# A graph attention layer's gather-and-sum: edge groups of 512 with 512-column products into separate sums, and softmax denominators by scans

## The chip, the cores and the metric

The kernel runs on one core of a Trainium2 chip. The metric is the device time of one execution in microseconds (us).

## The reference

Nodes have 1024 features in 4 heads of 256. 50,000 edges, sorted by their target node `dst`, run between N = 3125 nodes. The graph layer projects the normalised nodes (`xp`), gives each edge and head a softmax weight, and sums the weighted rows of the sources into their targets. A quantised linear layer follows.

```python
xp = (layernorm(x) @ W).reshape(N, H, C)                 # N=3125, H=4, C=256
e = leaky_relu(a_src[src] + a_dst[dst], 0.2)             # with self loops
m = segment_max(e, dst); ee = exp(e - m[dst])
z = segment_sum(ee, dst)                                 # the denominators
out = segment_sum(xp[src] * (ee / z[dst])[:, :, None], dst) + bias
x = x + relu(out)
x = x + (quantised layernorm(x)) @ (quantised weight).T + bias
```

## The kernel before

There are four stages, each a function with its own program for each engine. `normalise` and `project` make the tables; `aggregate` is the gather-and-sum; `finish` divides by the denominators and runs the linear layer. PE multiplies, DVE and ACT are the vector and scalar engines, POOL issues the gathers, SP issues plain transfers.

`project` writes `d_xp`, one row of 4 KB for each node: 1024 values in float16, and their rest in float16 (the high and the low part). It also makes the edges' weights in a layout with 128 edges on the partitions. Along the edges, it finds each node's largest logit with scans (line 1195 and 1201), writes them to `d_segmax`, and gathers them by node into `nmax` (`gather`, line 1022).

`aggregate` works on chunks of 128 edges. A step is 2 chunks, 256 edges in sorted order; there are 196 of them. Nodes come in 25 tiles of 128. A step whose edges cross from one tile to the next handles those of one tile only, and 24 border steps of one chunk each take the edges left over. So there are 220 steps and 416 chunks, in the order of `PLAN`: 6 border steps first, then a border step after every 10 others. For each chunk:

- POOL gathers 128 rows of `d_xp` into one of 12 buffers `xg` (line 1682). It waits until PE is done with that buffer (semaphore `mm_done`).
- DVE makes a one-hot matrix `hot` of the edges' targets (line 1701) and the low parts of the weights, `wgt` (line 1712); ACT makes the high parts (line 1757), 4 instructions a chunk.
- PE multiplies for each of 4 heads three pairs of parts, 256 columns each, all into the same sums `sum_ps` (line 1783): 12 products a chunk. At the end of a step it multiplies `hot` with the weights themselves, 8 columns, into `z_ps` (line 1793).

After each step DVE adds `z_ps` to the denominators `zsum` (line 1740) and `sum_ps` to the tile's rows in `acc` (line 1741). The queues of each engine are fixed by the order in the code; semaphores tie them together. `sum_ps` has 3 buffers, `z_ps` 2, `wgt` 3.

## Time and profile before

| what | value |
|---|---|
| median of 3 runs | 1515.13 us (1513.52 to 1517.62) |
| the profiled execution's own time | 1526.42 us |
| its span | 1524.7 us |
| main loop of `aggregate`: first product to last sum | 524.2 to 1211.9 us |
| first gather to the start of the last | 519.4 to 1197.6 us |
| granted TensorE clock, mean of the span | 0.96 |

A profile lists when each instruction started and how long it took, and what ended the wait before it. Busy shares of the engines over the whole span are PE 87%, DVE 71%, ACT 66%, POOL 44%. Instructions that issue a gather count as POOL's work. "issue" as the releaser means that the profile shows nothing that the engine waited for.

### The profile page before, as it was taken

The page shows a single profiled execution, that of the slowest core. Times are in us where ns is not written, and L with a number is a line of the kernel's source. Part 1 is how long each engine was busy: PE and PEld are TensorE (multiplying, and loading weights), DVE is VectorE, ACT ScalarE, POOL GpSimd, SP SyncE. Part 2 cuts the span into 40 slices and gives each one's busy share as a digit, 9 for nine tenths or more (in the row PEclk, how much of TensorE's full clock was granted, in tenths as well). Part 3 has the DMA queues.
Part 4 walks back from the last instruction along what each step waited for, and adds up shares of the span by engine and source line. Part 5 has one row for each costly group of instructions (what it writes and reads, how often), then busy time and mean ns, then how long its engine had stood idle before and what let it go on. Part 6 is the DMA issues. An engine that isn't in the chain of part 4 may idle for free. (4 is left out here: it accounts for less than half of the span.)

```text
span 1524.7 us, 29568 instructions
## 1 busy us (share of the span) xinstructions
PE 1327.2 (87%) x10150; PEld 902.0 (59%) x10150; DVE 1081.6 (71%) x2255; ACT 1006.7 (66%) x2253; POOL 672.7 (44%) x610
## 2 busy tenths in 40 slices
PE   7998577899997678889899988888998769999997
PEld 5775244554443367777677777776777634544543
DVE  7997489889833567666676666676676787777771
ACT  3667478885445467777777777776777665666652
POOL 1003411111255466666666566665666244443441
PEclk9999799999998899999999999999999979999999
DMA  6784475543463698988898998988888857767752
GB/s 233 275 297 134 138 251 184 181 157 119 152 215 111 235 317 313 317 310 299 305 309 307 309 349 303 316 301 292 306 309 300 306 162 189 195 173 195 188 141 48
DMA packets 110549, 363.62 MB, mean 238 GB/s; under 512 B 20204, under 2 KB 20988, under 8 KB 110148
## 3 DMA queue, kind: packets, MB, share of 16 engines
q0 software_dynamic: 66048, 225.15, 45.7%
q1 hardware_dynamic: 40996, 135.71, 26.0%
q8 instruction: 82, 1.34, 0.3%
q10 hardware_dynamic: 3360, 0.91, 0.2%
q14 instruction: 63, 0.52, 0.1%
HBM read 299.78 MB, written 72.85 MB: 244 GB/s over the span
## 5 line engine op out<-in xcount | busy, mean ns | idle before, releaser
L1783 PE MATMUL sum_ps<-xg,wgt 128*128 128x256 f16 x4992 | 602.5, 277 | 91.5 <-issue 66.8
L1757 ACT ACTIVATE wgt<-hot,tables 128x128 f16<-128x128 f16 x1664 | 503.0, 388 | 187.8 <-PE sum_ps L1783 61.5
L1783 PEld LDWEIGHTS sum_ps<-xg,wgt 128*128 128x128 f16 x4992 | 475.5, 99 | 185.3 <-issue 112.8
L1682 POOL DMA_INDIRECT xg<-d_xp,tables x404 | 414.1, 1025 | 243.9 <-issue 98.3
L1555 PE MATMUL xp_ps<-acc 128*128 128x512 f16 x1152 | 274.3, 387 | 21.7 <-issue 11.9
L1741 DVE TENSOR_TENSOR acc<-sum_ps,acc 128x1024 f32 x220 | 268.1, 1219 | 1.4 <-issue 1.3
L2180 PE MATMUL fmm_ps<-xg,tables 128*128 128x512 f16 x1200 | 265.0, 381 | 4.0 <-DVE tables L2009 4.0
L2180 PEld LDWEIGHTS fmm_ps<-xg,tables 128*128 128x128 f16 x1200 | 117.8, 98 | 141.8 <-issue 7.1
L1555 PEld LDWEIGHTS xp_ps<-acc 128*128 128x128 f16 x1152 | 108.9, 99 | 146.6 <-issue 28.5
L1740 DVE TENSOR_TENSOR zsum<-z_ps,zsum 128x8 f32 x220 | 35.5, 162 | 217.1 <-PE z_ps L1793 75.4
L1712 DVE TENSOR_TENSOR wgt<-hot,tables 128x512 f16<-128x512 f16 x416 | 157.8, 418 | 0.0
L1911 POOL TENSOR_TENSOR tables<-tables,finv 128x1024 f32<-128x1024 f32 x24 | 45.9, 1912 | 131.8 <-DVE finv L1997 131.8
L1059 POOL TENSOR_TENSOR acc<-acc,q_inv 128x1024 f32<-128x1024 f32 x8 | 17.3, 2157 | 176.1 <-DVE q_inv L1184 176.1
L1532 PEld LDWEIGHTS gat_ps<-table,oh 128*128 128x128 f16 x790 | 41.9, 99 | 60.4 <-issue 25.3
L1532 PE MATMUL gat_ps<-table,oh 128*128 128x100 f16 x790 | 48.8, 210 | 32.5 <-DVEq L1139 19.9
L1131 DVE TENSOR_TENSOR prod<-gat_ps,mask 128x500 f32<-128x500 f32 x79 | 53.2, 674 | 32.3 <-remote 19.4
L1424 ACT ACTIVATE acc<-xp_ps,half_scale 128x1024 f16<-128x1024 f32 x24 | 26.7, 1112 | 70.4 <-PE xp_ps L1555 61.3
L2021 DVE SCALAR_TENSOR_TENSOR tables<-ftr_ps,tables 128x1024 f16<-128x1024 f32 x24 | 29.4, 1225 | 53.1 <-ACT tables L2123 53.1
L1456 ACT ACTIVATE oh<-tables,back_lane 128x1280 f16<-128x1280 bf16 x40 | 54.0, 1351 | 16.0 <-remote 15.6
L1701 DVE TENSOR_TENSOR hot<-iota,tables 128x256 f16<-128x256 f16 (+1 forms) x220 | 59.8, 273 | 3.8 <-PEq L1767 3.7
L1917 POOL TENSOR_TENSOR tables<-fq,fscale 128x1024 f32<-128x1024 fp8e4 x24 | 53.9, 2244 | 14.9 <-ACT fq L2114 14.9
L1153 DVE SCALAR_TENSOR_TENSOR acc<-xp_ps,half_scale,acc 128x1024 f16<-128x1024 f32 x24 | 30.7, 1281 | 41.7 <-ACT acc L1425 24.7
(320 smaller groups left out, 1526.4 us busy)
## 6 DMA issues: line engine op xcount, KB each, us to landing
d_xnT<-acc SPq DMA_DIRECT2D x25, 512.0 KB, 3.6
tables<-d_lo SPq DMA_DIRECT2D x40, 320.0 KB
own_row<-d_own SPq DMA_DIRECT2D x25, 512.0 KB
wdT<-in_x_dram SPq DMA_DIRECT2D x24, 512.0 KB, 5.1
acc<-d_xnT SPq DMA_DIRECT2D x24, 512.0 KB
d_xp<-acc SPq DMA_DIRECT2D x24, 512.0 KB
d_own<-acc SPq DMA_DIRECT2D x24, 512.0 KB
xr<-in_x_dram SPq DMA_DIRECT2D x24, 512.0 KB
```

What stands on the lines that cost most here:

```text
L1131: return own.mark(nc.vector.tensor_tensor(out=prod[:, :, :, :], in0=gat_ps[u % 2][:, 0:UCOLS * V].rearrange("p (c h t) -> p c h t", c=UCOL ...
L1456: nc.scalar.activation(oh[at][:, :], digits[at], ACT.Abs, bias=back_lane[:, :]).then_inc(oh_ready, 1)
L1532: last = nc.tensor.matmul(gat_ps[u % 2][:, c * V:(c + 1) * V], oh[b % LB][:, col], table[a][:, :], start=(c == 0 and a == 0), stop=(c == U ...
L1555: done = nc.tensor.matmul(xp_ps[j][:, cols], xh[j][:, a, c, :], w16[:, c, b, cols], start=False, stop=(c == KC - 1 and a == 1), skip_group ...
L1682: nc.gpsimd.indirect_dma_start(out=xg[s][u][:, :, :].rearrange("p a n -> p (a n)"), out_offset=None, in_=d_xp, in_offset=bass.IndirectOffs ...
L1701: nc.vector.tensor_tensor(out=hot[k % TURN][:, 0:n, :].rearrange("p u (n b) -> p u n b", b=2), in0=iota16[:, :].rearrange("p (n b) -> p n ...
L1712: last = nc.vector.tensor_tensor(out=wgt[k % WB][:, u, HEADS:V, :].rearrange("p v (n b) -> p v n b", b=2), in0=hot[k % TURN][:, u, :].rear ...
L1741: nc.vector.tensor_tensor(out=s_acc, in0=sum_ps[k % SB][:, :], in1=s_acc, op=ALU.add).then_inc(added, 1)
L1757: last = nc.scalar.activation(wgt[k % WB][:, u, h, :], hot[k % TURN][:, u, :], ACT.Copy, scale=col(numT[:, h, :], u, q))
L1783: last = nc.tensor.matmul(sum_ps[s][:, h * C:(h + 1) * C], w[:, u, a * HEADS + h, :], x[u][:, b, h * C:(h + 1) * C], start=(u == 0 and h % ...
L1917: nc.gpsimd.tensor_tensor(out=blocks(xn[t % XN]), in0=blocks(q8[t % 2][:, :]), in1=spread(scale[t % XN][:, :]), op=ALU.mult).then_inc(xq_r ...
L2180: return nc.tensor.matmul(mm_ps[t % 2][:, cols], xqT[t % 2][:, a, c, :], wd[c][:, b, cols], start=False, stop=last, skip_group_check=True)
```

## The change

A step becomes a group of 4 chunks, 512 edges, worked in two parts of 2 chunks (`PARTS`). There are 98 groups. The 24 border pieces become one part each, so 2 chunks where it was 1. In all there are 220 parts and 440 chunks. For each head and chunk, one product of 512 columns takes the weights' high part with both parts of the row, into two separate sums; a second one of 256 columns takes the low part of the weights with the high part of the row. `sum_ps` is now 2048 columns with 2 buffers, and DVE adds both halves into `acc` once per group or border piece.

The products for the denominators and their adds are gone. Instead DVE runs sums along the edges in `project` (`line_sums`, `sum_carries`, `segment_sums`), SP writes them to `d_segsum`, and POOL gathers them by node in `aggregate`, 25 gathers of 16 bytes a row, one behind each of the parts 12 to 36.

```diff
@@ -32,7 +32,8 @@
 LAST_EVEN = LAST_ROWS // 16 * 16
-SUB = 2
+SUB = 4
+PAIR = 2
 ET = -(-E // (SUB * P))
 EC = ET * SUB
 EP = EC * P
@@ -40,14 +41,14 @@
 CROSSES = TILES - 1
 STEPS = ET + CROSSES
 LEAD = 6
-EVERY = 10
+EVERY = 5
 def sequence():
     plan, crosses = [(ET + j, 1) for j in range(LEAD)], LEAD
     for i in range(ET):
-        plan.append((i, SUB))
+        plan.append((i, SUB // PAIR))
         if i % EVERY == EVERY - 1 and crosses < CROSSES:
             plan.append((ET + crosses, 1))
             crosses += 1
@@ -55,8 +56,9 @@
 PLAN = sequence()
-assert len(PLAN) == STEPS and all(n == SUB for _, n in PLAN[-8:])
-KCOLS = 2 * P
+PARTS = [(step, q, w, n) for step, (q, n) in enumerate(PLAN) for w in range(n)]
+assert len(PLAN) == STEPS and all(n == SUB // PAIR for _, n in PLAN[-4:])
+KCOLS = P
 KT = STEPS
 HCOLS = 17
 HBATCH = 24
...
+    d_segsum = nc.dram_tensor("d_segsum", (EP, HEADS), F32, kind="Internal").ap()
...
+                if t == BUSY + 13:
+                    sp.wait_ge(sums_ready, 1)
+                    sp.dma_start(g["d_segsum"].rearrange("(p c) h -> p (c h)", c=EC),
+                                 segmax[:, :, :].rearrange("p c h -> p (c h)")).then_inc(segmax_out, 16)
...
+            sp.wait_ge(segmax_out, 32)
...
-            for c in range(CH):
-                for u in range(SUB):
-                    part = slice(u * P, (u + 1) * P)
-                    gather(srow[:, c, part], halves(d_src), step_i[:, c, u:u + 1], ends_in)
-                    gather(drow[:, c, part], halves(d_dst), step_i[:, c, u:u + 1], ends_in)
+            for part_no in range(SUB // PAIR):
+                part = slice(part_no * PAIR * P, (part_no + 1) * PAIR * P)
+                gather(srow[:, part], pairs(d_src), step_i[:, part_no:part_no + 1], ends_in)
+                gather(drow[:, part], pairs(d_dst), step_i[:, part_no:part_no + 1], ends_in)
             pool.wait_ge(tile_out, 16)
...
-            for c in range(CH):
-                for u in range(SUB):
-                    part = slice(u * P * HEADS, (u + 1) * P * HEADS)
-                    gather(nrow[c][:, part], halves(d_num), step_i[:, c, u:u + 1], rows_in)
+            for part_no in range(SUB // PAIR):
+                gather(w[:, part_no, :], pairs(d_num), step_i[:, part_no:part_no + 1], rows_in)
             highest(range(5, TILES))
...
+            def running_sums(start):
+                for h in range(HEADS):
+                    last = nc.vector.tensor_tensor_scan(segmax[:, :, h], same[:, :], edge[:, :, h], start(h), ALU.mult, ALU.add)
+                return last
+            def line_sums():
+                dve.wait_ge(num_ready, 1)
+                dve.wait_ge(steps_read, 1)
+                running_sums(lambda h: 0.0).then_inc(ends_ready, 1)
+            def sum_carries():
+                dve.wait_ge(sums_turned, 1)
+                own.link(nc.vector.tensor_copy(line_sum[:, 0, :], gat_ps[1][0:HEADS, 0:P]))
+                own.link(nc.vector.tensor_tensor_scan(line_sum[:, 1, :], joined[:, 1, :], line_sum[:, 0, :], 0.0, ALU.mult, ALU.add))
+                nc.vector.memset(line_sum[:, 0, 0:1], 0.0)
+                nc.vector.tensor_tensor(out=line_sum[:, 0, 1:P], in0=line_sum[:, 1, 0:P - 1], in1=joined[:, 0, 1:P],
+                                        op=ALU.mult).then_inc(cin_ready, 1)
+            def segment_sums():
+                dve.wait_ge(cinT_done, 2)
+                dve.wait_ge(sums_turned, 1)
+                own.link(nc.vector.tensor_copy(zcinT[:, :], g_ps[:, 0:HEADS]))
+                running_sums(lambda h: zcinT[:, h:h + 1]).then_inc(sums_ready, 1)
...
+                if t == BUSY + 8:
+                    line_sums()
+                if t == BUSY + 9:
+                    sum_carries()
...
                 if t == BUSY + 12:
                     num_pairs()
                     own_logits()
+                    segment_sums()
...
-    SB = 3
-    ROUND = 12
+    SB = 2
+    COUNT = len(PARTS)
...
-        sum_ps = [ps(f"sum_ps{j}", [P, D]) for j in range(SB)]
-        z_ps = [ps(f"z_ps{j}", [P, 512]) for j in range(2)]
+        hot = [sb(f"hot{j}", [P, PAIR, P], F16) for j in range(TURN)]
+        wgt = [sb(f"wgt{j}", [P, PAIR, V, P], F16) for j in range(WB)]
+        sum_ps = [ps(f"sum_ps{j}", [P, HEADS, 2, C]) for j in range(SB)]
...
+            for p in range(XB, COUNT):
+                gather(p)
+                if ZFROM <= p < ZFROM + TILES:
+                    t = p - ZFROM
+                    nc.gpsimd.indirect_dma_start(
+                        out=zsum[:, t, :], out_offset=None, in_=g["d_segsum"],
+                        in_offset=bass.IndirectOffsetOnAxis(ap=g["last_i"][:, t:t + 1], axis=0)).then_inc(g["z_in"], 16)
...
+            def add(p):
+                step, q, w, n = PARTS[p]
+                t = dve.value_load(tile_row[0:1, q:q + 1], min_val=0, max_val=TILES - 1)
+                dve.wait_ge(mm_done, PAIR * (p + 1 + TURN))
+                s_acc = acc[:, bass.ds(t, 1), :].rearrange("p o (h c) -> p (o h) c", h=HEADS)
+                for a in range(2):
+                    dve.wait_ge(added, 2 * (step + SB) + a)
+                    nc.vector.tensor_tensor(out=s_acc, in0=sum_ps[step % SB][:, :, a, :], in1=s_acc, op=ALU.add).then_inc(added, 1)
...
-            def turn(k):
-                if k + 3 < STEPS:
-                    one_hots(k + 3)
-                if k + 2 < STEPS:
-                    weights(k + 2)
-                t = dve.value_load(tile_row[0:1, PLAN[k][0]:PLAN[k][0] + 1], min_val=0, max_val=TILES - 1)
-                dve.wait_ge(mm_done, SUB * (k + 1 + TURN))
-                dve.wait_ge(added, k + SB)
-                dve.wait_ge(z_added, k + 2)
-                s_acc = acc[:, bass.ds(t, 1), :].rearrange("p o n -> p (o n)")
-                z_acc = zsum[:, bass.ds(t, 1), :].rearrange("p o n -> p (o n)")
-                nc.vector.tensor_tensor(out=z_acc, in0=z_ps[k % 2][:, 0:V], in1=z_acc, op=ALU.add).then_inc(z_added, 1)
-                nc.vector.tensor_tensor(out=s_acc, in0=sum_ps[k % SB][:, :], in1=s_acc, op=ALU.add).then_inc(added, 1)
-            for k in range(STEPS):
-                if k == LEAD:
+            for p in range(COUNT):
+                if p == LEAD:
                     dve.wait_ge(cleared, len(BEHIND))
-                turn(k)
+                if p + 3 < COUNT:
+                    one_hots(p + 3)
+                if p + 2 < COUNT:
+                    weights(p + 2)
+                step, q, w, n = PARTS[p]
+                if w == n - 1:
+                    add(p)
...
-            def step(k):
-                q, n = PLAN[k]
-                s, z, x, w = k % SB, k % 2, xg[k % XB], wgt[k % WB]
-                pe.wait_ge(arrived[k % XB], landed(k))
-                pe.wait_ge(added, k + 1)
-                pe.wait_ge(low_ready, k + 1)
-                for u in range(n):
-                    pe.wait_ge(high_ready, halves_to(k) + u + 1)
+            pe.sem_inc(mm_done, PAIR * TURN)
+            pe.sem_inc(added, 2 * SB)
+            def products(p):
+                step, q, w, n = PARTS[p]
+                s, x, wt = sum_ps[step % SB], xg[p % XB], wgt[p % WB]
+                pe.wait_ge(arrived[p % XB], landed(p))
+                if w == 0:
+                    pe.wait_ge(added, 2 * (step + 1))
+                pe.wait_ge(low_ready, p + 1)
+                for u in range(PAIR):
+                    pe.wait_ge(high_ready, PAIR * p + u + 1)
+                    first, final = w == 0 and u == 0, w == n - 1 and u == PAIR - 1
                     for h in range(HEADS):
-                        for i, (a, b) in enumerate(((0, 0), (0, 1), (1, 0))):
-                            last = nc.tensor.matmul(
-                                sum_ps[s][:, h * C:(h + 1) * C], w[:, u, a * HEADS + h, :],
-                                x[u][:, b, h * C:(h + 1) * C],
-                                start=(u == 0 and h % 2 == 0 and i == 0), stop=(u == n - 1 and h % 2 == 1 and i == 2),
-                                skip_group_check=True)
-                    if u == 0:
-                        last.then_inc(mm_done, 1)
-                pe.wait_ge(z_added, k + 1)
-                for u in range(n):
-                    last = nc.tensor.matmul(z_ps[z][:, 0:V], hot[k % TURN][:, u, :], numT16[:, u * KT + q, :, 0],
-                                            start=(u == 0), stop=(u == n - 1))
-                last.then_inc(mm_done, 1)
-            for k in range(STEPS):
-                step(k)
+                        cols = slice(h * C, (h + 1) * C)
+                        nc.tensor.matmul(s[:, h, :, :], wt[:, u, h, :], x[u][:, :, cols], start=first, stop=False, skip_group_check=True)
+                        last = nc.tensor.matmul(s[:, h, 0, :], wt[:, u, HEADS + h, :], x[u][:, 0, cols], start=False, stop=final,
+                                                skip_group_check=True)
+                    last.then_inc(mm_done, 1)
+            for p in range(COUNT):
+                products(p)
...
-            own.link(nc.vector.tensor_tensor(out=z32[:, :, :], in0=zsum[:, :, 0:HEADS], in1=zsum[:, :, HEADS:2 * HEADS], op=ALU.add))
-            own.link(nc.vector.scalar_tensor_tensor(out=z32[:, :, :], in0=z32[:, :, :], scalar=1.0 / NUM_SCALE,
-                                                    in1=self_num[:, :, :], op0=ALU.mult, op1=ALU.add))
+            own.link(nc.vector.tensor_scalar(has01[:, :], g["has"][:, :], 0.0, None, ALU.is_equal))
+            dve.wait_ge(g["z_in"], 16 * TILES)
+            own.link(nc.vector.tensor_tensor(out=z32[:, :, :], in0=zsum[:, :, :],
+                                             in1=has01[:, :].unsqueeze(2).to_broadcast([P, TILES, HEADS]), op=ALU.mult))
+            own.link(nc.vector.tensor_tensor(out=z32[:, :, :], in0=z32[:, :, :], in1=self_num[:, :, :], op=ALU.add))
```

On PE, a step of before in the middle of `aggregate` (`sum_ps0` is a buffer of the sums, `xg0_0` and `xg0_1` the rows of its two chunks):

```order
L1783 MATMUL sum_ps0<-xg0_0,wgt0 128x256 x12
L1783 MATMUL sum_ps0<-xg0_1,wgt0 128x256 x12
L1793 MATMUL z_ps0<-tables,hot0 128x8 x2
L1783 MATMUL sum_ps1<-xg1_0,wgt1 128x256 x12
L1783 MATMUL sum_ps1<-xg1_1,wgt1 128x256 x12
```

And of the changed kernel, the end of a group's last chunk and the first chunk of the next group:

```order
L1827 MATMUL sum_ps0<-xg0_1,wgt0 128x512
L1828 MATMUL sum_ps0<-xg0_1,wgt0 128x256
L1827 MATMUL sum_ps1<-xg1_0,wgt1 128x512
L1828 MATMUL sum_ps1<-xg1_0,wgt1 128x256
L1827 MATMUL sum_ps1<-xg1_0,wgt1 128x512
L1828 MATMUL sum_ps1<-xg1_0,wgt1 128x256
L1827 MATMUL sum_ps1<-xg1_0,wgt1 128x512
L1828 MATMUL sum_ps1<-xg1_0,wgt1 128x256
L1827 MATMUL sum_ps1<-xg1_0,wgt1 128x512
L1828 MATMUL sum_ps1<-xg1_0,wgt1 128x256
L1827 MATMUL sum_ps1<-xg1_1,wgt1 128x512
L1828 MATMUL sum_ps1<-xg1_1,wgt1 128x256
```

A chunk has 8 products in place of 12, and the products with `tables` are gone. Each product has a load of its own weights, which isn't listed here.

On DVE, one step of before (`TENSOR_LOAD` reads the tile's number; `ISA` sets addresses):

```order
L1741 ISA
L1741 TENSOR_TENSOR acc<-sum_ps2,acc 128x1024
L1701 TENSOR_TENSOR hot0<-iota16,tables 128x256
L1712 TENSOR_TENSOR wgt2<-hot3,tables 128x512 x2
L1733 TENSOR_LOAD tile_row
L1733 ISA x2
L1740 ISA
L1740 TENSOR_TENSOR zsum<-z_ps1,zsum 128x8
L1741 ISA
L1741 TENSOR_TENSOR acc<-sum_ps0,acc 128x1024
```

And one group of the changed kernel:

```order
L1746 TENSOR_TENSOR hot1<-iota16,tables 128x256
L1757 TENSOR_TENSOR wgt1<-hot0,tables 128x512 x2
L1746 TENSOR_TENSOR hot2<-iota16,tables 128x256
L1757 TENSOR_TENSOR wgt2<-hot1,tables 128x512 x2
L1767 TENSOR_LOAD tile_row
L1767 ISA x2
L1772 ISA
L1772 TENSOR_TENSOR acc<-sum_ps0,acc 128x1024 x2
```

The small add is gone, and two adds of 1024 columns stand behind two parts in place of one behind each step.

On POOL, before, gathers 35 to 41 of `aggregate`:

```order
L1682 DMA xg1_0<-d_xp,tables 128x2048
L1682 DMA xg1_1<-d_xp,tables 128x2048
L1682 DMA xg2_0<-d_xp,tables 128x2048
L1682 DMA xg2_1<-d_xp,tables 128x2048
L1682 DMA xg3_0<-d_xp,tables 128x2048
L1682 DMA xg3_1<-d_xp,tables 128x2048
L1682 DMA xg4_0<-d_xp,tables 128x2048
```

And the changed kernel at parts 12 to 14, where the gathers of the denominators stand between those of the rows:

```order
L1722 DMA xg0_0<-d_xp,tables 128x2048
L1722 DMA xg0_1<-d_xp,tables 128x2048
L1735 DMA zsum<-d_segsum,last_i 128x4
L1722 DMA xg1_0<-d_xp,tables 128x2048
L1722 DMA xg1_1<-d_xp,tables 128x2048
L1735 DMA zsum<-d_segsum,last_i 128x4
L1722 DMA xg2_0<-d_xp,tables 128x2048
L1722 DMA xg2_1<-d_xp,tables 128x2048
L1735 DMA zsum<-d_segsum,last_i 128x4
```

One gather of 4 columns has come in behind each two gathers of 2048 columns, 25 in all.

## Rows read from the trace of the kernel before

**Rows 1.** Busy time in one stretch, with its header; inside the main loop.

```profile
core 0: us, PE busy (x) PEld busy (x) DVE busy (x) ACT busy (x) POOL busy (x), PEclk, DMA share, GB/s
560.00:1200.00 640.00, 567.02 (x5118) 475.81 (x5117) 437.97 (x1015) 475.87 (x1575) 402.09 (x393) 0.98 0.90 310
```

**Rows 2.** Groups, 524 to 1211 us: count | busy us, mean ns | idle before, its releasers.

```profile
L1783 PE MATMUL sum_ps<-xg,wgt 128*128 128x256 f16 x4992 | 602.5, 277 | 91.5 <-issue 66.8 <-DMA xg<-d_xp,first_idx 11.1 <-DVE wgt L1712 8.1
L1757 ACT ACTIVATE wgt<-hot,tables 128x128 f16<-128x128 f16 x1652 | 499.4, 388 | 183.0 <-PE sum_ps L1783 61.5 <-remote 47.7 <-PE z_ps L1793 45.2
...
L1682 POOL DMA_INDIRECT xg<-d_xp,tables x404 | 414.1, 1025 | 243.9 <-issue 98.3 <-PE sum_ps L1783 72.7 <-PE z_ps L1793 60.1
L1741 DVE TENSOR_TENSOR acc<-sum_ps,acc 128x1024 f32 x220 | 268.1, 1219 | 1.4 <-issue 1.3
L1712 DVE TENSOR_TENSOR wgt<-hot,tables 128x512 f16<-128x512 f16 x414 | 157.0, 418 | 0.0
L1701 DVE TENSOR_TENSOR hot<-iota,tables 128x256 f16<-128x256 f16 (+1 forms) x217 | 59.3, 273 | 0.0
```

**Rows 3.** Line 1682, the gathers: their durations, and what ended POOL's idle time.

```profile
L1682 POOL DMA_INDIRECT xg<-d_xp,tables x404: 984/990/1437, 532.7 to 1197.6; - x135
L1682 POOL DMA_INDIRECT xg<-d_xp,first_idx x12: 986/990/1174, 519.4 to 547.5; - x12
...
  issue: 101.4, 311
  PE sum_ps L1783: 72.7, 52
  PE z_ps L1793: 60.4, 45
...
  remote: 12.7, 7
```

**Rows 4.** Timeline of PE and POOL, 821 to 829 us.

```profile
822.14 0.92 PE L1783 MATMUL sum_ps<-xg,wgt 128*128 128x256 f16 x7
...
823.93 1.10 POOL L1682 DMA_INDIRECT xg<-d_xp,tables  x1 [0.30 <-issue]
...
824.73 0.27 PE L1783 MATMUL sum_ps<-xg,wgt 128*128 128x256 f16 x1 [0.47 <-issue]
...
826.13 3.15 PE L1783 MATMUL sum_ps<-xg,wgt 128*128 128x256 f16 x14 [1.14 <-issue]
...
826.94 0.99 POOL L1682 DMA_INDIRECT xg<-d_xp,tables  x1 [1.91 <-PE sum_ps L1783]
```

**Rows 5.** Timeline, 458 to 486 us, the end of a row of gathers in the stage before.

```profile
465.44 0.38 PE L1555 MATMUL xp_ps<-acc 128*128 128x512 f16 x1 [0.35 <-issue]
...
472.26 0.94 POOL L1022 DMA_INDIRECT nmax<-d_segmax,last_i  x1 [0.30 <-issue]
...
474.66 5.59 PE L1555 MATMUL xp_ps<-acc 128*128 128x512 f16 x18 [1.51 <-issue]
```

**Rows 6.** Timeline, 798 to 835 us, one undisturbed step on PE.

```profile
803.04 2.78 PE L1783 MATMUL sum_ps<-xg,wgt 128*128 128x256 f16 x24
...
805.71 2.56 PE L1783 MATMUL sum_ps<-xg,wgt 128*128 128x256 f16 x22
```

**Rows 7.** Timeline, 486 to 520 us: the last tile of the stage before.

```profile
502.53 10.52 PE L1545 MATMUL xp_ps<-acc 128*128 128x512 f16 x48
```

**Rows 8.** Groups of instructions, 350 to 520 us.

```profile
L1022 POOL DMA_INDIRECT nmax<-d_segmax,last_i x25 | 25.4, 1016 | 7.5 <-issue 7.3
L1153 DVE SCALAR_TENSOR_TENSOR acc<-xp_ps,half_scale,acc 128x1024 f16<-128x1024 f32 x13 | 16.6, 1278 | 40.1 <-ACT acc L1425 24.7 <-issue 15.3
...
L1195 DVE TENSOR_TENSOR_SCAN segmax<-fences,asrc 128x392 f32<-128x392 f32 x4 | 5.2, 1356 | 0.0
```

**Rows 9.** The page: costliest groups, the products of the last stage.

```profile
L2180 PE MATMUL fmm_ps<-xg,tables 128*128 128x512 f16 x1200 | 265.0, 381 | 4.0 <-DVE tables L2009 4.0
```

**Rows 10.** DMA issues: size, and median us from issue to landing.

```profile
d_segmax<-segmax SPq DMA_DIRECT2D x1, 784.0 KB, 6.0
```

More of the change, by code:

```diff
@@ L266, in normalise @@
     CH = KCOLS // P
-    MIDDLES = (P, ET - 1 - P)
     XS = 4
@@ L1232, in carries @@
                 own.link(nc.vector.tensor_tensor(out=whole, in0=erow[:, 1, :], in1=erow[:, 2, :], op=ALU.is_equal))
+                nc.vector.tensor_copy(joined[:, 0, :], joins)
+                own.link(nc.vector.tensor_tensor(out=joined[:, 1, :], in0=whole, in1=joins, op=ALU.mult))
                 own.link(nc.vector.tensor_scalar(whole, whole, -1.0, BIG, ALU.add, ALU.mult))
@@ L1801, in finish @@
+            for p in range(COUNT):
+                products(p)
 def finish(nc, maker, g):
```

202 lines of the change are left out of this document (101 added, 101 removed).

## The prediction

> **What bounds the kernel now.** I read the stages first. The change is felt in `aggregate`, whose main loop runs from 524 to 1212 us, 45% of the span. In its undisturbed part no engine is full and the DMA engines are busy 0.90 of the time [rows 1]: PE 567 of 640 us, ACT 476, DVE 438, POOL 402. So the next question is who waits for whom.
>
> PE's own work is short of the time. One undisturbed step starts at 803.04 and the next one 2.67 us later [rows 6], that is 1.335 us a chunk and 555 us for 416 chunks. The loop takes 687 us. The missing 130 us are mostly "issue" in the groups: PE was idle before products, and the profile names nobody [rows 2]. Waits for gathered rows or for weights are small there (11.1 and 8.1 us).
>
> The timeline shows what such a pause looks like [rows 4]. From 822.14 PE does 7 products at full speed, then only single ones (one of them at 824.73), and at 826.13 it is back at work. POOL began its last gather at 823.93 and ended it at 825.03; then it waited for PE, since all 12 buffers were in use. PE came back 1.1 us after POOL had fallen silent. That could be chance, so I looked for a long row of gathers where POOL doesn't wait for PE. There is one in `project` [rows 5]: with products of 512 columns PE crawls in the same way, the last gather ends at 473.20, and PE is back at 474.66, 1.5 us later. So I read it thus: while POOL issues gathers with hardly a break, PE runs out of something after a while, and it goes on only after a break of more than 1 us. In `aggregate` the break comes about when PE's standstill has filled the buffers.
>
> This makes POOL's queue the loop's clock. From the first gather at 519.4 to the end of the last at 1198.6 are 679 us [rows 3]: 416 gathers at 1.025 us [rows 2] are 426, the pauses of about 0.3 us between them 101, the 104 waits for PE 146 (72.7 + 60.4 + 12.7, mean 1.40), and memsets the rest. A wait comes once in 4 chunks.
>
> **The change part by part.**
>
> *PE.* A chunk was 12 products of 256 columns and one small product, each with its load of weights. Now it is 8 products, 4 of them of 512 columns. The trace has 512 columns at 10.52 us for 48 [rows 7], about 0.216 us each, and 256 columns at 2.78 us for 24 [rows 6], 0.109 each with the tail taken off. So a chunk costs 4 x 0.325 = 1.30 us in place of 1.335, and 440 chunks cost 572 us in place of 555: PE loses 17 us of its own. This isn't added to the sum, as POOL sets the pace; it would count only if the gathers got out of the way.
>
> *POOL, rows.* The border pieces take two chunks each, so there are 24 more gathers. Most of their rows are left out, but the instruction is the same: 24 x 1.025 = 24.6 us.
>
> *POOL, denominators.* The 25 new gathers stand in the same queue. Their like are those of `nmax`, which also have 16 bytes a row: 25 took 25.4 us [rows 8]. I take that: +25.4. All stand behind parts 12 to 36, when POOL has no lead yet. There POOL needs 3 gathers for a part, some 3.9 us, and PE needs 2.6 for it.
>
> *POOL, waits.* Here I choose. If a standstill comes after so many instructions of PE, it comes less often: 3520 products instead of 5408, 0.65 of them, so 68 waits in place of 104. I keep their 1.40 us, since a wait holds the 1.1 us that PE needs after the last gather and the time to its first finished chunk. That saves 36 x 1.40 = 50.5 us. The gathers not behind a wait number 397 in place of 311 and bring 86 x 0.30 = 25.8 us of pauses. Bounds: no waits left (-146 us), or as many per chunk as now (110 waits, +8).
>
> For the stage: 24.6 + 25.4 - 50.5 + 25.8 = +25 us. With W waits the whole is -48 + 1.10 W, with `project` below in it: even at W = 43.
>
> *DVE and ACT.* ACT needs 499.4/1652 = 0.302 us for each of 1760 instructions, 532 us in a loop of about 710 [rows 2]. DVE has 440 low weights of 0.38 (157.0/414), 220 one-hots of 0.27 (59.3/217), and 244 adds of 1.22 us: 524 us. The second add makes a group cost 4.5 us, PE's part of it 5.2, so it is hidden. At a border piece it isn't: 3.5 us against PE's 2.6, with only 2 buffers. POOL's two gathers there take 2.65 us. If that were exposed at each of 24 it would be 20 us; since a group behind it gives 0.7 us back and PE stands still anyway, I take nothing and keep 20 for the range.
>
> *project.* Eight scans more on DVE, 1.0 to 1.36 us each [rows 8], four early in one tile's time and four in another's. DVE has 40.1 us of idle time before 13 instructions there, 3.1 us a tile [rows 8]; a set of four costs at most 5.4 us, so up to 2 us could be late each time. The tables are 488 wide and not 440, which is below 1 us for each of 8 passes. The new store of 784 KB goes out just ahead of the last rows of `d_xp`, for which `aggregate` waits; its like took 6.0 us to land [rows 10]. Four gathers of indices fewer lie in POOL's idle time. I take +2 us for all; bounds 0 and 10.
>
> *finish.* Three small operations on DVE become four, and the wait on the 25 gathers has long been met. Nothing.
>
> The sum is +27. Against the profiled execution that is 1526.4 + 27 = 1553 us. The median of the runs lies 11 us under that execution, and with the same gain or loss comes to 1542 us.
>
> **The rivals.**
>
> *The waits all but go (chance 0.16).* PE now takes in 16 instructions in 1.30 us, 12 a us, where it was 26 in 1.335, 19 a us. If the gathers leave it a trickle that is enough for 12, there is no standstill. For this: in the last stage 1200 products of 512 columns have 4.0 us of idle time [rows 9]. Against: POOL issues few DMAs there, and in `project` PE stood still with 512 columns too [rows 5]. It would give -48 us, 1467. This is the case on the other side; it decides from W = 43 down.
>
> *Something between (0.24).* W between 30 and 55, or the new gathers fall into waits that come anyway, which takes 25.4 + 25 x 0.30 = 33 us off: -15 to +13, so 1500 to 1528. Against the latter: PE comes back only when POOL is silent, so a gather put into a wait makes it longer.
>
> *Main case (0.46).* W from 55 to 80: +13 to +40, 1528 to 1555.
>
> *The waits go with the gathers, not with PE's instructions (0.14 with DVE's 20 us exposed).* W = 110 gives +73, 1588. For this: the profile names no shortage, and POOL's waits are also plain full buffers.
>
> The Trainium skill speaks for this last one: in "Runtime: NRT & Kernel Launch", "Instruction fetch mechanics", it says that each engine's instructions come in blocks of 256, fetched while the block before is worked, and that the cost of a boundary is mostly hidden. By that rule PE would not run short of instructions, and fewer of them would save no wait. Rows 4 and 5 show PE short of something while no semaphore holds it, and don't show of what.
>
> **How the numbers follow.** The predicted time is the main case's, 1542. Its own range is 1528 to 1555. The range for 8 in 10 leaves out the far end of the first rival and the far end of the last: 1482 to 1572. A measurement of this kernel tells about 0.3%, 4.5 us, from no change. Faster by more: the first rival and half of the second, 0.28. Within: 0.10. Slower: 0.62.
>
> **What would show it.** The gathers of the rows and the new ones should keep 1.0 us each, and stand at 0.3 us from each other. POOL's waits for PE should number about 68 in all, of 1.4 us; this count decides between the cases. Between parts 12 and 36 POOL should hardly wait, and PE should have idle time before its products. PE's products should take 1.30 us a chunk where undisturbed. DVE should wait for PE in each group. I am wrong if POOL's waits fall below 43 or stay above 90, if PE doesn't come back about 1 us after POOL's last gather, if PE waits for DVE's adds at the border pieces, or if the last store delays the first gather by more than 5 us.

## The result, and the profile after

The changed kernel takes 1559.7 us (median of 4 runs, 1557.1 to 1561.83), the kernel before 1514.33 (4 runs, 1513.13 to 1517.62). The ratio is 1.0295, with an interval of 1.0272 to 1.0318: 45 us slower. The forecast was 1542, slower, with a range up to 1572.

The profiled execution of the changed kernel took 1561.83 us, its span is 1560.1. That of before took 1526.42, 12 us above its own median, so the two traces differ by 35.4 us of span only. These 35.4 us can be placed. Here are the groups of `aggregate`'s loop, the costliest first (line, engine, operation, count; busy time in us and mean ns; idle time in us ahead of them and who ended it):

```profile
L1827 PE MATMUL sum_ps<-xg,wgt 128*128 128x512 f16 x1760 | 606.2, 392 | 102.8 <-issue 43.4 <-DVE wgt L1757 37.1 <-DMA xg<-d_xp,first_idx 15.4
...
L1828 PE MATMUL sum_ps<-xg,wgt 128*128 128x256 f16 x1760 | 493.0, 280 | 12.2 <-issue 12.0
L1722 POOL DMA_INDIRECT xg<-d_xp,tables x428 | 442.0, 1033 | 220.0 <-issue 111.4 <-PE sum_ps L1828 91.5 <-remote 17.1
L1772 DVE TENSOR_TENSOR acc<-sum_ps,acc 128x1024 f32 x243 | 297.1, 1223 | 155.0 <-PE sum_ps L1828 111.2 <-remote 35.2 <-issue 4.1
...
L1735 POOL DMA_INDIRECT zsum<-d_segsum,last_i x25 | 24.2, 966 | 7.6 <-issue 7.3 <-PE sum_ps L1828 0.3
```

And POOL's gathers of rows and of denominators by themselves, with what they waited for (us, times):

```profile
L1722 POOL DMA_INDIRECT xg<-d_xp,tables x428: 984/990/1261, 537.2 to 1229.7; - x143
L1722 POOL DMA_INDIRECT xg<-d_xp,first_idx x12: 986/990/1121, 516.2 to 530.7; - x12
its engine sat idle before it (us, times) until:
  issue: 114.7, 361
  PE sum_ps L1828: 91.5, 69
  POOLq L846: 21.1, 1
  remote: 17.1, 9
...
L1735 POOL DMA_INDIRECT zsum<-d_segsum,last_i x25: 958/962/1065, 557.5 to 663.4; - x25
its engine sat idle before it (us, times) until:
  issue: 7.3, 24
  PE sum_ps L1828: 0.3, 1
```

POOL's loop runs from 516.2 to 1230.8, 714.6 us, against 679.2 of before [rows 3]. The whole difference of 35.4 us lies there. The first gather comes 3.2 us earlier, and what follows the loop takes 3.2 us more. Within the loop:

| term | predicted | in the traces | from |
|---|---|---|---|
| 24 more gathers of rows | +24.6 | +27.7 | 440 at 1.03 against 416 at 1.025 |
| 25 gathers of denominators | +25.4 | +24.2 | 25 at 0.966 |
| pauses of 0.3 us | +25.8 | +20.6 | 114.7 + 7.3 against 101.4 |
| POOL's waits for PE | -50.5 (68 waits) | -36.9 (79 waits) | 91.5 + 17.1 + 0.3 against 145.8 |
| sum | +25.3 | +35.6 | |

So the gathers cost what was expected. What is missing is part of the gain. In the early part, with three gathers for a part, PE gets through 52 chunks (417 products) in 105 us; without the 25 gathers, in e1 below, it does 67 there (535). Later the loop looks much as before (busy us of PE, PEld, DVE, ACT and POOL with instructions, clock, DMA share and GB/s; PEld is PE's load of weights). The changed kernel, then the kernel before:

```profile
560.00:665.00 105.00, 82.41 (x417) 42.50 (x416) 54.23 (x103) 61.20 (x202) 71.65 (x72) 0.88 0.72 229
800.00:950.00 150.00, 132.59 (x789) 76.34 (x788) 106.96 (x199) 116.73 (x392) 99.86 (x98) 0.99 0.89 317
```

```profile
560.00:665.00 105.00, 93.25 (x846) 78.11 (x845) 73.56 (x172) 79.03 (x263) 66.71 (x66) 0.98 0.92 317
800.00:950.00 150.00, 132.90 (x1205) 111.90 (x1203) 102.09 (x238) 110.53 (x368) 92.79 (x92) 0.98 0.91 318
```

### The profile page after: what moved, and what is told of

The parts are those of the page before. It is cut to its first block and busy times, and to the rows that moved or that the text cites. A ratio compares the mean times of both kernels' runs of the same rounds, so it can differ in the third digit from the quotient of the medians.

```text
span 1560.1 us, 24997 instructions
## 1 busy us (share of the span) xinstructions
PE 1345.5 (86%) x8264; PEld 745.5 (48%) x8264; DVE 1115.0 (71%) x2096; ACT 1034.8 (66%) x2349; POOL 719.2 (46%) x653
## 5 line engine op out<-in xcount | busy, mean ns | idle before, releaser
L1827 PE MATMUL sum_ps<-xg,wgt 128*128 128x512 f16 x1760 | 606.2, 392 | 102.8 <-issue 43.4
L1802 ACT ACTIVATE wgt<-hot,tables 128x128 f16<-128x128 f16 x1760 | 530.0, 387 | 197.3 <-PE sum_ps L1828 108.6
L1722 POOL DMA_INDIRECT xg<-d_xp,tables x428 | 442.0, 1033 | 220.0 <-issue 111.4
L1828 PE MATMUL sum_ps<-xg,wgt 128*128 128x256 f16 x1760 | 493.0, 280 | 12.2 <-issue 12.0
L1772 DVE TENSOR_TENSOR acc<-sum_ps,acc 128x1024 f32 x244 | 298.3, 1223 | 155.0 <-PE sum_ps L1828 111.2
L1827 PEld LDWEIGHTS sum_ps<-xg,wgt 128*128 128x128 f16 x1760 | 176.4, 100 | 347.3 <-issue 142.9
L1828 PEld LDWEIGHTS sum_ps<-xg,wgt 128*128 128x128 f16 x1760 | 176.5, 100 | 41.8 <-issue 18.3
L1757 DVE TENSOR_TENSOR wgt<-hot,tables 128x512 f16<-128x512 f16 x440 | 165.7, 418 | 0.0
L1746 DVE TENSOR_TENSOR hot<-iota,tables 128x256 f16<-128x256 f16 x220 | 62.2, 284 | 83.6 <-PE sum_ps L1828 45.5
L2059 DVE SCALAR_TENSOR_TENSOR tables<-ftr_ps,tables 128x1024 f16<-128x1024 f32 x24 | 29.4, 1224 | 53.6 <-ACT tables L2161 53.6
```

What stands on the lines that cost most here:

```text
L1722: nc.gpsimd.indirect_dma_start(out=xg[s][u][:, :, :].rearrange("p a n -> p (a n)"), out_offset=None, in_=d_xp, in_offset=bass.IndirectOffs ...
L1746: nc.vector.tensor_tensor(out=hot[p % TURN][:, :, :].rearrange("p u (n b) -> p u n b", b=2), in0=iota16[:, :].rearrange("p (n b) -> p n b" ...
L1757: last = nc.vector.tensor_tensor(out=wgt[p % WB][:, u, HEADS:V, :].rearrange("p v (n b) -> p v n b", b=2), in0=hot[p % TURN][:, u, :].rear ...
L1772: nc.vector.tensor_tensor(out=s_acc, in0=sum_ps[step % SB][:, :, a, :], in1=s_acc, op=ALU.add).then_inc(added, 1)
L1802: last = nc.scalar.activation(wgt[p % WB][:, u, h, :], hot[p % TURN][:, u, :], ACT.Copy, scale=numT[:, h, at:at + 1])
L1827: nc.tensor.matmul(s[:, h, :, :], wt[:, u, h, :], x[u][:, :, cols], start=first, stop=False, skip_group_check=True)
```

## The experiments

There were three sets; each kernel is compared with the kernel before as it ran in its own set. It took 1514.1 us in the first, 1526.8 in the second, and 1382.1 in the third (median of 13 runs, 1378.6 to 1387.2). The program was the same each time. Where sets are compared, ratios stand, or times worked out from them for the first set's 1514 us; that a change costs the same share in each set is taken for granted there, and the third set shows that it can fail. What is different in the third set is told at its end.

### First set: one part of the change undone

**e1: no gathers of denominators.** `zsum` is set to 1 in their place, so the sums are divided by other numbers than they should be.

```diff
-                if ZFROM <= p < ZFROM + TILES:
-                    t = p - ZFROM
-                    nc.gpsimd.indirect_dma_start(
-                        out=zsum[:, t, :], out_offset=None, in_=g["d_segsum"],
...
+                if p == ZFROM:
+                    nc.gpsimd.memset(zsum[:, :, :], 1.0).then_inc(g["z_in"], 16 * TILES)
```

> The changed kernel with the 25 gathers of the denominators left out (zsum is filled with ones by one memset, so the output isn't the reference's). Theory A, POOL's queue is the clock of the loop: 25 gathers of 0.97 us and their pauses of 0.3 us go, 32 us less, less what comes back as waits for PE: 1528 to 1545 us. Rival B, the new gathers stand where POOL would have waited anyway: no change, 1555 to 1562 us.

Measured: 1527.45 us (1522.96 to 1530.16), ratio 1.0084 (1.0056 to 1.0112). That is 32 us below the changed kernel: 25 gathers cost 1.29 us each, their 0.97 and a pause of 0.30. POOL's waits stayed as they were, 77 with 107 us in place of 79 with 109. The queue is simply shorter.

**e2: the products of 512 columns as two of 256.** All else stays as in the changed kernel.

```diff
-                        nc.tensor.matmul(s[:, h, :, :], wt[:, u, h, :], x[u][:, :, cols], start=first, stop=False, skip_group_check=True)
+                        for b in range(2):
+                            nc.tensor.matmul(s[:, h, b, :], wt[:, u, h, :], x[u][:, b, cols], start=first and b == 0, stop=False,
+                                             skip_group_check=True)
```

> The changed kernel with each product of 512 columns issued as two of 256, so 12 products a chunk in place of 8, with the same result and nearly the same work of PE (12 x 0.109 = 1.31 us a chunk in place of 1.30). Theory A, PE runs short after so many of its own instructions and needs a silence of POOL: waits of POOL for PE rise from 79 to about 118, and at 1.1 us each this is +43 us: 1590 to 1610 us. Rival B, the waits go with chunks, bytes or DVE's and ACT's pace: +4 us, 1560 to 1568 us.

Measured: 1576.17 us (1572.85 to 1579.71), ratio 1.0419 (1.0392 to 1.0447), 16.5 us above the changed kernel and so between the two expectations. Who waited for whom, in the loop (us, times, longest):

```profile
POOL xg L1722 <- PE sum_ps L1830: 93.1, 63, 4.2
PE sum_ps L1828 <- issue: 69.8, 99, 4.0
POOL xg L1722 <- remote: 36.0, 22, 2.4
...
PE sum_ps L1830 <- issue: 19.8, 38, 1.1
PE sum_ps L1828 <- DVE wgt L1757: 10.8, 15, 1.5
```

The same view of the changed kernel:

```profile
PE sum_ps L1827 <- issue: 43.4, 42, 4.0
PE sum_ps L1827 <- DVE wgt L1757: 37.1, 27, 3.2
...
PE sum_ps L1828 <- issue: 12.0, 21, 1.6
```

With 12 products a chunk PE is idle without a named releaser 137 times and 90 us; with 8 it is 63 times and 55 us. Before, with 12 and the small one, its products had 66.8 us of such idle time [rows 2]. These pauses do go by PE's instructions. POOL's waits follow by less: 86 with 129 us, against 79 with 109, where theory A had 118 waits. Those 20 us, less 6 us of pauses between gathers, are the 15 us by which POOL's loop is longer.

**e3: one chunk in place of two in 18 of the 24 border pieces.** The edges of the second chunk there are left out of the sums. The loops over `PAIR` of POOL, DVE, ACT and PE run once for them.

```diff
+        short = lambda p: p >= XB and PARTS[p][3] == 1
...
-                for u in range(PAIR):
+                for u in range(1 if short(p) else PAIR):
```

> The changed kernel with the second chunk left out of 18 of the 24 border pieces, gather, weights and products (its edges are missing from the output). Theory A: 18 gathers of 1.33 us less and 18 x 16 instructions of PE less (2 waits): about -26 us, 1530 to 1538 us. Rival B, the border pieces cost through DVE's two adds, which stay: -5 to +5 us. It is not told apart from A if the adds and the gathers both count; then between.

Measured: 1541.21 us (1533.7 to 1542.51), ratio 1.0187 (1.0169 to 1.0206), 18.5 us below the changed kernel for 18 chunks: 1.03 us each, less than the gather and its pause, and just above theory A's range. The execution in the trace took 1533.7 us, less than the median: POOL's loop in it is 689.1 us, 25.5 below 714.6, or 1.42 us a chunk. Rival B alone, no change, is out; how A and B share it isn't shown. PE's waits for DVE's weights fell from 37.1 us to 29.4, but waits for its adds came up, 19.2 us in 5.

**e4: the kernel before with breaks in POOL's queue.** If PE comes to a standstill until POOL is silent, a short silence on purpose should be cheaper than filled buffers. The memset covers 896 columns of float16, behind each 4 chunks' gathers.

```diff
             for k in range(XB, STEPS):
                 gather(k)
+                chunks += PLAN[k][1]
+                if chunks >= 4:
+                    chunks = 0
+                    nc.gpsimd.memset(pause[:, :], 0.0).then_inc(paused, 1)
+                    breaks += 1
+                    pool.wait_ge(paused, breaks)
```

> The kernel of before with one memset of 896 float16 columns on POOL after each 4 chunks' gathers, about 100 breaks of 0.6 to 1.2 us. Theory A, PE's standstills end only in a silence of POOL: PE's pauses (126 us in the loop) shrink to less than half, POOL's waits for PE (104) mostly go, and the time moves little, -20 to +10 us: 1495 to 1525 us. Rival B, POOL's silence is only the consequence of PE's pauses: these stay at 104 to 126 us, the breaks come on top where POOL had no wait: +30 to +80 us.

Measured: 1541.25 us (1540.6 to 1542.62), ratio 1.0187 (1.0168 to 1.0206). PE's unnamed pauses all but went, as theory A had it, and yet the time rose by 27 us. The chief waits of PE and what POOL does (timeline of POOL: start, length, and the idle time ahead in brackets):

```profile
PE sum_ps L1793 <- DMA xg<-d_xp,tables: 89.1, 103, 5.1
...
PE sum_ps L1793 <- issue: 7.6, 12, 2.3
```

```profile
822.56 0.87 POOL L1700 MEMSET pause<- 128x896 f16 x1
824.19 0.99 POOL L1684 DMA_INDIRECT xg<-d_xp,tables  x1 [0.77 <-PE z_ps L1803]
825.49 1.00 POOL L1684 DMA_INDIRECT xg<-d_xp,tables  x1 [0.30 <-issue]
826.80 1.10 POOL L1684 DMA_INDIRECT xg<-d_xp,tables  x1 [0.30 <-issue]
828.21 0.99 POOL L1684 DMA_INDIRECT xg<-d_xp,tables  x1 [0.30 <-issue]
829.20 0.86 POOL L1700 MEMSET pause<- 128x896 f16 x1
```

From memset to memset are 6.64 us for 4 chunks: 4.08 of gathers, 0.87 of memset, 0.77 behind it and 0.90 of pauses. POOL does not stand anywhere; the 0.77 is the same with PE or with the memset as its releaser, so it is no true wait. PE now takes each row as it lands. A break with its gap takes 0.87 + 0.77 us, and 98 of them come to 160 us, in place of 146 us of waits for PE. The loop of 689 us is POOL's own work: 426 of gathers, 90 of memsets, and 174 of gaps. It is 10 us longer than in the trace of before; of the other 17 us, 12 lie between that trace and the median beside it. Theory A was right on the standstills and wrong on the time, at most 1525 us, since a break takes more of POOL's time than the memset alone. The run doesn't part POOL's silence from PE's own stops, though: PE now stood 103 times waiting for rows.

### Second set: position, bytes, and the border pieces

**e5: 2 KB a row in place of 4, as many gathers.**

```diff
-                        out=xg[s][u][:, :, :].rearrange("p a n -> p (a n)"), out_offset=None, in_=d_xp,
+                        out=xg[s][u][:, 0, :], out_offset=None, in_=d_xp.rearrange("n (a c) -> (n a) c", a=2),
```

> The changed kernel, with 2 KB gathered for each edge in place of 4 KB, in as many gathers; the other half of each row buffer is set to zero once, before the first gather (12 memsets), so the low parts of the rows are left out of the sums and wrong rows are taken. PE's, DVE's and ACT's work is unchanged. Theory Q (POOL's queue is the clock: issue time, pauses of 0.3 us and PE's standstills; bytes don't matter): the gathers still take 1.03 us each and stand 0.31 us apart, the loop of POOL stays between 695 and 725 us, and the time between 1545 and 1570 us. Rival D (the DMA engines, busy 0.89 of the loop, are the bound, and PE's standstills come from their being full): the standstills with no named releaser fall to less than half, and the time is below 1510 us.

Measured: 1576.62 us (1576.41 to 1580.35), ratio 1.0329 (1.0308 to 1.0351); the changed kernel's ratio is 1.0295. The expectations of this set were written with the first set's 1514 us in mind; at that level 1.0329 is 1564 us, as theory Q had it, and POOL's loop of 722 us lies in its range. Rival D wanted less than half of the unnamed pauses; there are 104 us of them, more than the changed kernel's 55. The DMA engines are less busy, and POOL goes at the same pace:

```profile
800.00:950.00 150.00, 135.43 (x776) 78.43 (x777) 106.50 (x200) 115.82 (x383) 98.63 (x97) 0.94 0.59 169
```

97 gathers against 98 in the same 150 us, with 169 GB/s in place of 317. A gather of 128 rows took 1.036 us on POOL with 2 KB rows, 1.033 with 4 KB and 0.966 with 16 bytes. The bytes don't count here, the number of gathers does.

**e6: the denominators' gathers one behind every 8th part.**

```diff
-                if ZFROM <= p < ZFROM + TILES:
-                    t = p - ZFROM
+                if p >= ZFROM and (p - ZFROM) % 8 == 0 and (p - ZFROM) // 8 < TILES:
+                    t = (p - ZFROM) // 8
```

> The changed kernel, with the 25 gathers of the denominators behind every 8th part from part 12 on, in place of one behind each of the parts 12 to 36. Theory Q (each takes its 0.97 us and a pause in the queue that is the loop's clock, wherever it stands): 1553 to 1563 us, POOL's loop 708 to 720 us. Rival L (they cost so much because they stand close together where POOL has no lead over PE): spread out, most go into waits for PE, 1530 to 1545 us, POOL's loop below 700 us.

Measured: 1568.19 us (1567.24 to 1568.88), ratio 1.0268 (1.0251 to 1.0285), 1555 us at the first set's level. Its interval and that of the changed kernel overlap. POOL's loop is 722.8 us, 3 above theory Q's range and far from the 700 of rival L. Where the gathers stand matters little; rival L is out.

**e7: the second add of a group one part later.**

```diff
-                if w == n - 1:
-                    add(p)
+                if p > 0 and PARTS[p - 1][2] == PARTS[p - 1][3] - 1:
+                    add(p - 1, 1)
+                if PARTS[p][2] == PARTS[p][3] - 1:
+                    add(p, 0)
```

> The changed kernel, with the second of the two adds of a group or border piece moved one part later on DVE (behind the next part's one-hots and weights), so that no part has more than about one extra add in front of the weights that follow, the border pieces too. Theory Q (PE's 37 us of waits for DVE's weights at the border pieces lie inside the loop that POOL's queue sets): those waits fall below 15 us, and the time stays within 8 us of 1560. Rival B (they are additional): 1520 to 1545 us.

Measured: 1573.41 us (1572.74 to 1577.91), ratio 1.031 (1.0287 to 1.0333). PE's chief waits in the loop:

```profile
PE sum_ps L1828 <- issue: 69.2, 50, 10.7
...
PE sum_ps L1828 <- DVE acc L1771: 24.1, 10, 3.4
...
PE sum_ps L1829 <- issue: 8.2, 16, 1.0
```

The waits for DVE's weights are gone. In their place are 24.1 us for its adds, so the waits for DVE aren't below the 15 us that were expected, and the unnamed pauses are 77 us. The changed kernel itself didn't run in this set, but e6 did, in which DVE's order is the same: there PE's unnamed pauses are 67 us, its waits for DVE 34 and for ACT 5, 106 in all, and here they are 77, 24 and 3, 104. The ratio is that of the changed kernel. So DVE's lateness at the border pieces isn't an addition. What PE doesn't wait for DVE, it waits otherwise.

**e8: the kernel before with 25 small gathers more.**

```diff
                 gather(k)
+                if 2 * XB <= k < 2 * XB + TILES:
+                    t = k - 2 * XB
+                    nc.gpsimd.indirect_dma_start(
+                        out=more[:, t, :], out_offset=None, in_=g["d_segmax"],
+                        in_offset=bass.IndirectOffsetOnAxis(ap=first_idx[:, 0, 0:1], axis=0)).then_inc(more_in, 16)
```

> The kernel before, with 25 more gathers of 16 bytes a row behind steps 12 to 36, into a tile that nobody reads. PE, DVE and ACT are unchanged. Theory Q: each takes about 0.97 us and a pause of 0.31 us in the queue, 32 us in all: 1540 to 1553 us. Rival H (with 4 buffers of waits for PE in the queue they go into waits that come anyway): 1512 to 1528 us.

Measured: 1562.46 us (1558.61 to 1564.11), ratio 1.0221 (1.0199 to 1.0242): 36 us more, 1.43 each, and 1548 us at the first set's level. POOL's loop is 711.9 us, 32.7 above the 679.2 of before. The same price holds in the other kernel:

```profile
L1697 POOL DMA_INDIRECT more<-d_segmax,first_idx x25 | 25.5, 1022 | 7.6 <-issue 7.0 <-PE z_ps L1801 0.6
```

### Third set: bytes and breaks in the kernel before

**e0: the kernel before once more.**

> The kernel before once more, to see how far its profiled execution and its loop differ from chip to chip: a POOL loop of 665 to 685 us, 98 to 110 waits for PE.

Measured: 1382.69 us, span 1381.0, and neither number of the expectation held. POOL's loop is 565.4 us, from 484.6 to 1050.0, where it was 679.2. The chief waits of POOL for PE and of PE in it:

```profile
POOL xg L1682 <- issue: 118.7, 386, 0.6
PE sum_ps L1783 <- DMA xg<-d_xp,tables: 7.7, 6, 2.3
POOL xg L1682 <- PE z_ps L1793: 7.4, 13, 2.8
POOL xg L1682 <- PE sum_ps L1783: 3.0, 10, 0.3
```

```profile
800.00:950.00 150.00, 150.00 (x1463) 134.53 (x1462) 126.82 (x290) 135.54 (x451) 113.17 (x110) 1.00 0.98 372
```

PE has no unnamed pause in the loop. It is busy for all of the 150 us, with 1463 products where [rows 1] have PE idle for a tenth of the time. POOL issues 110 gathers there, one in 1.36 us. A gather takes 1.03 us as ever, and its pause 0.3. This is the same program on the same inputs with its standstills gone. Of the 144 us between the two spans 114 lie in the loop, and 35 in the stages ahead of it, whose end is the first gather (484.6 against 519.4); what follows the loop takes 5 us more.

**e9: the kernel before with rows of 2 KB.** The edit is that of e5.

> The kernel before, with 2 KB gathered for each edge in place of 4 KB, in as many gathers, and 12 memsets of the other halves of the row buffers ahead of the first gather (about 11 us on POOL). The low parts of the rows are left out of the sums, and wrong rows are taken. Theory Q (POOL's queue and PE's standstills pace the loop before too, bytes don't matter): POOL's waits for PE number 95 to 110, and its loop from first to last gather stays within 670 to 690 us, the time 0 to 15 us above the kernel before. Rival D (the loop before is held by the rate of the transfers, 317 GB/s): POOL's loop below 650 us and the time at least 20 us below the kernel before.

Measured: 1382.33 us (1381.35 to 1387.46), ratio 1.0004 (0.9988 to 1.002). PE is again busy for all of the 150 us from 800 on, with the DMA engines busy 0.66 of it in place of 0.98. Rival D, that transfers hold the loop before, is out in this condition: it wanted 20 us. (The 12 memsets put the first gather 10 us later, so the halved bytes may have given back up to 10.) The first theory's numbers (95 to 110 waits) failed for the reason given under e0.

**e10: e4 and e9 together.**

> The kernel before with the breaks of e4 (one POOL memset behind each 4 chunks' gathers) and the rows of 2 KB of e9; the low parts of the rows are left out of the sums, and wrong rows are taken. In e4 PE had no more standstills without a named releaser and waited 89 us for rows to land. Theory D4 (what took their place in e4 is the rate of the transfers): PE's waits for rows fall below 20 us, POOL's loop is 640 us or less, and the time is 20 us or more below e4's 27 us above the kernel before. Rival Q4 (it is POOL's queue, memsets and all): the loop stays above 675 us, and the time within 10 us of e4 beside what the 12 memsets add.

Measured: 1507.61 us (1504.73 to 1508.49), ratio 1.0893 (1.086 to 1.0926).

```profile
PE sum_ps L1797 <- DMA xg<-d_xp,tables: 96.3, 82, 4.1
```

Half the bytes leave PE waiting for rows as long as in e4, so theory D4 is out: the landings were late because POOL issued them late. POOL's loop is 685.4 us from the first gather at 495.2 to the end of the last at 1180.6, above the 675 of rival Q4, and near e4's 689 although the sets differ. Q4's other sign, a time within 10 us of e4, can't be read across the sets. Where PE doesn't stand still, breaks cost 125 us and give back nothing.

**e11: breaks in the changed kernel,** 3 memsets of 300 columns of float16 behind each 8 chunks' gathers.

```diff
                 gather(p)
+                if p % 4 == 3:
+                    for _ in range(3):
+                        nc.gpsimd.memset(pause[:, :], 0.0).then_inc(cleared, 1)
+                        breaks += 1
+                        pool.wait_ge(cleared, len(BEHIND) + breaks)
```

> The changed kernel, with three POOL memsets of 300 columns (0.9 us in all) behind each 8 chunks' gathers, about as often as PE comes to a standstill there. Theory S (a standstill lasts as long as POOL takes to fill the 12 buffers, so a short break at the right time saves PE more than it costs POOL): PE's idle time without a named releaser falls to less than half of the 43 us, POOL's waits for PE fall by more than the 50 us that the memsets take, and the time is 10 to 30 us below the changed kernel. Rival Q (the breaks only take the place of waits or add to them): the time is 0 to 35 us above the changed kernel.

Measured: 1528.39 us (1528.06 to 1529.88), ratio 1.105 (1.1019 to 1.108) to the kernel before of this set. PE's unnamed pauses fell to 1.5 us in 3, and it waited 100.3 us for rows. Whether that is better than the changed kernel itself can't be said, as the changed kernel ran in no set of this condition. The time is 31 us below 1560, like theory S's 10 to 30, but not for its reason: POOL's loop, 487.4 to 1193.5, is 706 us, only 8.5 below the changed kernel's 714.6, and 29 us lie ahead of the first gather, where the edit changes nothing.

## Why the prediction was right in sign and short in size

*POOL's queue is the loop's clock: right under the condition of the first two sets.* The whole difference of the traces lies in POOL's loop. Gathers cost 1.3 to 1.4 us each, taken out (e1) or added to the kernel before (e8), and moving them (e6) or halving their bytes (e5) gave nothing back.

*More gathers: right.* 24.6 and 25.4 were predicted, 27.7 and 24.2 are in the traces. e1 and e3 confirm them in the time: 32 us for the denominators, and 1.03 us for a border chunk, so about 25 for 24 of them.

*Pauses: near enough,* +25.8 against +20.6, fewer because more waits were left.

*Waits: the term that was mis-sized.* The prediction said: "0.65 of them, so 68 waits in place of 104", and a gain of 50.5 us. There are 79, and the gain is 37 us. Their mean of 1.38 us was right. (With 79 waits in place of 68 the prediction's own formula gives +39 for the whole, in place of +27.) What failed in it is that waits go by the number of PE's instructions. Between the two PE forms, e2 gives 86 waits with 129 us against 79 with 109. PE's unnamed pauses did fall in number (137 and 63 in these two, 127 before), but they grew longer: from 0.54 us in the mean and 1.4 at most before to 0.88 and 3.96 in the changed kernel. And POOL's waits are not these pauses alone: each delay of PE fills the buffers. In the changed kernel 37 us of PE's delays are waits for DVE's weights, near border pieces. The prediction named waits for DVE's adds there as a thing that would prove it wrong. Those are 2.5 us; it is the weights queued behind the adds that came late. But e7 shows that taking most of it away gains nothing, since PE's idle time stays the same in all (104 us against 106 in e6).

By times: the changed kernel less 32 (denominators) less 25 (border chunks) is 1503, 12 us below the kernel before of 1514. Undoing the wide products cost 16.5 us in e2. So PE's new form is worth 12 to 17 us, where the prediction had 25 (50.5 less 25.8 of pauses). With the 1.42 us of e3's trace for a border chunk it would be 21.

*From trace to median: a step that failed too.* In the traces the loop came out 10 us above the terms. Another 10 us lie between the traces, which differ by 35.4, and the medians, which differ by 45.4; with the 2 us of `project` that didn't come, this is the 18 us between +27 and +45. The prediction let the difference against the profiled execution stand for the median. But that execution took as long as the kernel before in the second set (1526.8), not as in the first (1514.1) or beside the changed kernel (1514.3). Which waits it had more isn't settled: there is no trace of the kernel before at 1514 us.

*project: predicted +2, and the first gather came 3.2 us earlier* in the traces. The last store didn't delay the first gather by the 5 us that would have counted against the prediction.

*PE comes back about 1 us after POOL's last gather: only partly right.* An example of the changed kernel, POOL's timeline, and PE's around its return:

```profile
715.85 0.99 POOL L1722 DMA_INDIRECT xg<-d_xp,tables  x1 [0.30 <-issue]
717.30 0.99 POOL L1722 DMA_INDIRECT xg<-d_xp,tables  x1 [0.46 <-issue]
720.20 0.98 POOL L1722 DMA_INDIRECT xg<-d_xp,tables  x1 [1.91 <-remote]
```

```profile
715.03 0.27 PE L1828 MATMUL sum_ps<-xg,wgt 128*128 128x256 f16 x1
719.26 0.58 PE L1827 MATMUL sum_ps<-xg,wgt 128*128 128x512 f16 x1 [3.96 <-issue]
719.64 0.42 PE L1828 MATMUL sum_ps<-xg,wgt 128*128 128x256 f16 x1
719.86 0.63 PE L1827 MATMUL sum_ps<-xg,wgt 128*128 128x512 f16 x1
```

POOL fell silent at 718.29, PE was back at 719.26. Elsewhere PE comes back while POOL is issuing. Of its 30 unnamed pauses over 0.9 us before, 19 ended 0.8 to 1.2 us after POOL fell silent; in the changed kernel it is 3 of 19. This was one of the prediction's signs of being wrong, and it came. That PE's unnamed pauses need POOL's gathers is supported by e4, where breaks took them from 66.8 us to 7.6, with the reservation made there. That they are in the nature of the kernel is refuted by e0, where POOL issued faster than ever and PE never paused.

*The rival in which instruction blocks are fetched behind the work.* "Runtime: NRT & Kernel Launch", "Instruction fetch mechanics", of the Trainium skill says that the cost of a boundary is mostly hidden. The traces agree. They hold the time of every transfer of 16 KB on the instruction queue q8, whose number goes with PE's instructions (82 before, 80 in e2, 67 in the changed kernel). In POOL's loop there are 44 before, of 0.96 us in the median, and 44 in e0, of 0.97, where PE has no unnamed pause. Of the 127 pauses before, 8 have such a transfer under way, 4 of 69 us. So the pauses are not waits for these transfers. Nor are they waits for rows that the profile failed to name: at eleven of them before, looked at by the packets, 6 to 9 chunks of rows more had landed than PE had used. They aren't random either. PE often ran some 61 products of 256 columns between two groups of pauses before, and some 80 in e2:

```profile
816.70:822.80 6.10, 6.10 (x61) 5.46 (x61) 5.17 (x12) 6.01 (x21) 4.12 (x5) 1.00 0.90 314
```

```profile
868.20:876.80 8.60, 8.58 (x77) 7.44 (x77) 5.58 (x12) 7.78 (x26) 6.28 (x6) 1.00 0.91 318
```

So no single number of instructions sets them off, and what PE lacks in them isn't shown.

*What stays open.* What makes the standstills come in two sets and stay away in the third isn't known. One more thing differs: the traces of the first two sets hold only about two thirds of the semaphore events of those of the third (8353 landings before, 12651 in e0), so who ended a wait is less sure in them; that PE was idle is not. With the standstills away, the kernel before is held by PE (416 chunks of 1.335 are 555 us, POOL's loop is 565), and the changed kernel would need 465 gathers of 1.33 us on POOL, 618 us. POOL's loop in e11 fits that: 706 us less 89 for its 54 breaks is 617. By this estimate the changed kernel would lose about 53 us there. That wasn't tried.

No version here was faster than the kernel before in its set.

## What to carry to other kernels

Find the queue that sets the pace and count its instructions, not their bytes: here each small gather of 16 bytes a row cost as much as one of 4 KB a row, 1.3 us, and 49 more gathers outweighed all that wider products gave back. Don't price the removal of a wait by the instructions that seem to cause it. When one delay of an engine goes, another can take its place, as in e7. And run the kernel before again in each set of measurements: the pauses that this prediction took as given were absent in a later one.

## What the runs showed of the hardware that wasn't expected

- The same program took 1514, 1527 and 1382 us in three sets. The difference is in PE's unnamed pauses and POOL's waits: 104 waits with 146 us in the trace of before, 23 with 10 us in that of the third set.
- An indirect gather of 128 rows kept POOL 1.03 us with rows of 4 KB or 2 KB, and 0.97 us (changed kernel) to 1.02 (e8) with 16 bytes, and it took 0.30 us more until the next one. Behind a memset and its semaphore the next gather began 0.77 us later (e4).
- After a pause of 3.96 us in the changed kernel (above), PE came back with products of 512 columns at 0.63 us in place of 0.38. The granted clock of the stretch was 0.50, the 1.2 GHz level, for 6 us:

```profile
719.00:725.00 6.00, 5.74 (x19) 2.66 (x20) 4.68 (x11) 4.15 (x14) 3.00 (x3) 0.50 0.96 356
```
